# Embedding lookup and pairwise interaction: halves of 128 samples, wider lookups of nine tables, gram in two column tiles

## The reference, cut to what matters

```python
e = jnp.stack([tbl_0[ids[:, 0]], ..., tbl_26[ids[:, 26]]], axis=1)      # 2048 x 27 x 128
interactions = jnp.einsum('bfd,bgd->bfg', e, e)
x = interactions.reshape(B, F * F)[:, TRIL_IDX]                        # 351 pairs, i > j
h = jnp.concatenate([r_bottom_mlp_out, x, r_bottom_mlp_out], axis=1)     # 607 columns
h = jnp.maximum(h @ W_top1 + b_top1, 0.0)                              # 607 x 512
h = jnp.maximum(h @ W_top2 + b_top2, 0.0)                              # 512 x 256
y = h @ W_top3                                                         # 256 x 1
```

## Time and profile before

| | us |
|---|---|
| median of 3 runs | 481.43 (474.8 to 484.29) |
| the profiled execution | 476.27 |
| its span, first to last instruction | 474.5 |
| TensorE busy | 377.0 |
| GpSimd busy | 311.6 |
| VectorE busy | 255.4 |
| ScalarE busy | 155.2 |
| mean granted clock of TensorE | 0.939 of full |

### The profile page before, as it was taken

One profiled execution on the slowest core, in us unless ns is written; L12 is line 12 of the kernel. 1 busy time (PEld: TensorE's weight loads), 2 busy tenths in 40 slices (PEclk: granted clock), 3 DMA queues, 4 the chain that ended last, 5 costly groups with the idle time before them and its releaser, 6 DMA issues.

```text
span 474.5 us, 9001 instructions
## 1 busy us (share of the span) xinstructions
PE 377.0 (79%) x3732; PEld 343.9 (72%) x3732; DVE 255.4 (54%) x577; ACT 155.2 (33%) x199; POOL 311.6 (66%) x324
## 2 busy tenths in 40 slices
PE   0360686899898989898889889988989898976717
PEld 0360676888797879887788788878978797856616
DVE  0672863974498348835593549542974488310310
ACT  1312044224431453044404432333324531331411
POOL 5777557877777777777777777777777777720000
PEclk9965797999999999999999999998999999997967
DMA  6457512132224222422242222322242222210000
GB/s 157 152 178 205 162 32 71 42 133 68 67 67 137 67 66 64 141 68 62 63 143 59 66 69 74 128 65 71 65 136 66 67 67 59 67 37 4 1 16 0
DMA packets 24817, 38.69 MB, mean 82 GB/s; under 512 B 9436, under 2 KB 17125, under 8 KB 24776
## 3 DMA queue, kind: packets, MB, share of 16 engines
q0 software_dynamic: 10240, 20.99, 15.6%
q1 hardware_dynamic: 14536, 17.12, 12.1%
HBM read 35.00 MB, written 0.01 MB: 74 GB/s over the span
## 4 chain that ended last, share of the span: by engine, by line
PE 36%; DVE 24%; DMA 12%; issue 11%; POOL 10%; ACT 4%; SPq 3%; DVEq 0%
DVE mask L422 19%; PE gram_bank L531 11%; POOL rows L203 10%; PE mlp_bank L545 7%; PE col_bank L492 6%; DMA pairs<-in_tbl 6%; PE col_bank L506 6%; PE mlp_bank L556 5%; DVE pairs L455 3%; DMA rows<-in_tbl,idx 3%; SPq L229 3%; DMA rowid<-in_row_of_chunk 2%; ACT eT L322 2%; ACT pairs L334 1%; DVE eT L446 1%
## 5 line engine op out<-in xcount | busy, mean ns | idle before, releaser
L203 POOL DMA_INDIRECT rows<-in_tbl,idx x320 | 311.4, 973 | 107.1 <-issue 104.2
L492 PE MATMUL col_bank<-mask,parts 125*128 125x256 f32 x896 | 120.9, 294 | 49.8 <-DVE mask L422 48.4
L492 PEld LDWEIGHTS col_bank<-mask,parts 125*128 125x128 f32 x896 | 114.7, 200 | 57.0 <-issue 53.7
L422 DVE TENSOR_SCALAR mask<-hot_f,rowid 125x256 fp32r<-125x256 f16 x448 | 136.5, 374 | 0.1
L531 PE MATMUL gram_bank<-eT 128*58 128x52 f32 x2048 | 117.9, 218 | 13.5 <-issue 9.3
L531 PEld LDWEIGHTS gram_bank<-eT 128*58 128x58 f32 x2048 | 114.0, 135 | 19.9 <-issue 14.8
L446 DVE COPY eT<-col_bank 128x512 f32<-128x512 f32 x56 | 59.1, 1055 | 84.1 <-PE col_bank L506 81.3
L322 ACT ACTIVATE eT<-col_bank 128x512 f32<-128x512 f32 (+1 forms) x56 | 55.2, 986 | 148.1 <-PE col_bank L492 106.3
L455 DVE COPY pairs<-gram_bank 26x416 f32<-26x416 f32 x64 | 55.4, 865 | 84.6 <-PE gram_bank L531 84.1
L334 ACT ACTIVATE pairs<-gram_bank 26x416 f32<-26x416 f32 x64 | 56.8, 887 | 83.2 <-PE gram_bank L531 82.8
L545 PE MATMUL mlp_bank<-x,w 126*128 126x256 f32 (+5 forms) x288 | 64.0, 378 | 15.3 <-DMA x<-pairs 15.3
(11 more groups left out here) (10 smaller groups left out, 10.6 us busy)
## 6 DMA issues: line engine op xcount, KB each, us to landing
hot_i<-in_hot_ids SPq DMA_DIRECT2D x8, 896.0 KB
rows<-in_tbl,idx POOLq DMA_INDIRECT x320
pairs<-in_tbl SPq DMA_DIRECT2D x7, 500.0 KB
x<-in_bottom SPq DMA_DIRECT2D x8, 128.0 KB
x<-pairs SPq DMA_DIRECT2D x16, 39.0 KB
x<-pairs SPq DMA_DIRECT2D x16, 34.5 KB
w<-in_w SPq DMA_DIRECT2D x1, 512.0 KB
w<-in_w_pairs SPq DMA_DIRECT2D x2, 252.0 KB
```

The lines of the kernel that those rows point to most:

```text
L203: pool.indirect_dma_start(out=rows[:, h, n * D:(n + 1) * D], out_offset=None, in_=tables[f], in_offset=bass.IndirectOffsetOnAxis(ap=idx[:, ...
L422: last = nc.vector.tensor_scalar(mask[0:ROWS, k % MASKS, c, :], hot_f[0:ROWS, k, :], rowid[0:ROWS, c:c + 1], None, ALU.is_equal)
L492: last = nc.tensor.matmul(col_bank[b][:, i * TILE:(i + 1) * TILE], parts[0:ROWS, k, part, c * D:(c + 1) * D], mask[0:ROWS, k % MASKS, c, : ...
```

## The change

The unit of work becomes the half of 128 samples. Nine tables are looked up by TensorE (eight of 1000 rows and one of 1250, ten chunks), 18 are gathered. A lookup covers up to 512 samples, so each table is looked up once in four halves; its result goes to `eH`, and ScalarE places each half's columns from there into `eT`, which now holds one half. Two or three tables are looked up per half, in turn. In the front the lookups are 128 to 512 samples wide.

The ring of gathered rows is released group by group. All ids of the gathers come in one load, those of the lookups one table at a time. There are three column banks and three gram banks. The first half's transposes stand between the last five front lookups. A gram set is two strips of 16 samples, alternately at output partitions 0 and 64; VectorE copies strip 0, ScalarE strip 1, with the inner loop along samples, and the transposed groups are copied with the inner loop along tables. `pairs` and `x` are laid out by halves, so a transfer to x has runs of 1536 bytes. A table is loaded as 112 and 13 rows. At the end the last two halves' layers are interleaved, and half of the last transfers to x are issued from ScalarE. Layers 1 and 2 otherwise stay in tiles of 256.

The diff, cut to its core:

```diff
-ONE_HOT = 7
...
+ROWS = 125
+SMALLEST = [f for f in range(F) if VOCAB[f] == 8 * ROWS]
+NEXT = [f for f in range(F) if VOCAB[f] == 10 * ROWS]
+HOT_TABLES = SMALLEST[:2] + NEXT[:1] + SMALLEST[2:]
+HOT = len(HOT_TABLES)
+GATHERED_TABLES = [f for f in range(F) if f not in HOT_TABLES]
 GATHERED = len(GATHERED_TABLES)
-ORDER = GATHERED_TABLES + ONE_HOT_TABLES
-TILE = 256
-TILES = B // TILE
+ORDER = HOT_TABLES + GATHERED_TABLES
+CHUNKS = [VOCAB[f] // ROWS for f in HOT_TABLES]
 HALF = 128
-CHUNKS = 8
...
+HALVES = B // HALF
+TILE = 2 * HALF
+WINDOW = 4
+WIDE = WINDOW * HALF
+OWN = [[0, 1, 2], [3, 4], [5, 6], [7, 8]]
 PARTS = 2
-MASKS = 4
+PIECE = 2
+PIECES = [n // PIECE for n in CHUNKS]
+MASKS = 8
+SLOTS = 3
 STAGES = 3
 PAD = 32
...
 PACK = 2
-SET = 32
+GRAM_ROWS = (PACK - 1) * PAD + F - 1
+COLUMNS = 64
+STRIPS = 128 // COLUMNS
+STRIP = 16
+SET = STRIPS * STRIP
 SETS = HALF // SET
-GROUP = 4
 X_CHUNKS = 3
...
+SPLIT = 112
...
+GROUPS = spread(GATHERED, 4)
+NG = len(GROUPS)
+RING = 2 * NG
...
+LAST = HALVES - 1
...
+BANKS = 3
...
+LOOKUPS = [(k, 0, m + 1) for m in range(WINDOW) for k in OWN[m]]
+FRONT = len(LOOKUPS)
+AFTER = []
+for h in range(LAST):
+    AFTER.append([len(LOOKUPS) + i for i in range(len(OWN[h % WINDOW]))])
+    LOOKUPS += [(k, h + 1, min(WINDOW, LAST - h)) for k in OWN[h % WINDOW]]
...
+EARLY = FRONT - NG
...
+FRONT_ORDER = [("lookup", n) for n in range(EARLY)]
+for g in range(NG):
+    FRONT_ORDER += [("transpose", 0, g), ("lookup", EARLY + g)]
...
+def on_scalar(fill):
+    return fill < len(FRONT_ORDER) or fill % 2 == 1
...
+        def transposed(h, g):
+            n = transpose_fill(h, g)
+            return eT[:, :, HOT + GROUPS[g][0]:HOT + GROUPS[g][0] + GROUPS[g][1]], \
+                col_bank[n % BANKS][:, 0:GROUPS[g][1] * HALF].rearrange("p (f s) -> p s f", s=HALF)
...
+        def pairs_of(s, t, j):
+            a = s * SET + t * STRIP
+            return pairs[0:F - 1, :].rearrange("p (g s) -> p g s", s=HALF)[:, :, a + j:a + STRIP:PACK]
+        def gram_of(b, t, j):
+            row = COLUMNS * t + PAD * j
+            return gram_bank[b][row:row + F - 1, :, j * (F - 1):(j + 1) * (F - 1)].rearrange("p q g -> p g q")
...
+            pool.wait_ge(idx_loaded, 16)
+            for h in range(HALVES):
+                for g, (first, size) in enumerate(GROUPS):
+                    before = h * NG + g - RING
+                    if before >= 0:
+                        n = transpose_fill(before // NG, before % NG)
+                        pool.wait_ge(col_full[n % BANKS], n // BANKS + 1)
+                    for i in range(size):
+                        f = first + i
+                        pool.indirect_dma_start(
+                            out=rows_of(h, g)[:, i * D:(i + 1) * D], out_offset=None, in_=tables[GATHERED_TABLES[f]],
+                            in_offset=bass.IndirectOffsetOnAxis(ap=idx[:, h, f:f + 1], axis=0),
+                        ).then_inc(gathered[(h * NG + g) % RING], 16)
...
+            def load_table(k):
+                src = tables[HOT_TABLES[k]].rearrange("(p c) d -> p (c d)", c=CHUNKS[k])
+                for a, b in ((0, SPLIT), (SPLIT, ROWS)):
+                    sp.dma_start(stage_of(k)[a:b, :], src[a:b, :]).then_inc(table_loaded[k % STAGES], 16)
...
+            def load_x(h, blocks):
+                for b in range(BANKS):
+                    sp.wait_ge(gram_copied[b], STRIPS * used((h + 1) * SETS, b))
+                for r in blocks:
+                    out, src = x_block(h, r)
+                    sp.dma_start(out, src).then_inc(x_loaded[h % 2], 16)
...
+            for h in range(HALVES):
+                for n in CASTS[h] if h < LAST else ():
+                    if n + 2 < len(LOOKUPS):
+                        load_hot_ids(n + 2)
+                if h % 2 == 0:
+                    load_bottom(h // 2)
+                    if h >= 4:
+                        store_y(h // 2 - 2)
...
+                load_x(h, range(0, len(BLOCKS), 2) if h == LAST else range(len(BLOCKS)))
+            store_y(TILES - 1)
...
+            def place_hot(h, m):
+                at, first, last = (h - m - 1) % WINDOW * HALF, OWN[m][0], OWN[m][-1] + 1
+                return nc.scalar.activation(eT[:, :, first:last].rearrange("p s f -> p f s"),
+                                            eH[:, first:last, at:at + HALF], ACT.Copy)
+            def place_early(h):
+                for b in range(BANKS):
+                    act.wait_ge(gram_full[b], used(h * SETS, b))
+                for m in range(WINDOW):
+                    if m != (h - 1) % WINDOW:
+                        place_hot(h, m)
...
+                if h < LAST:
+                    copy_lookup(AFTER[h][0])
+                copy_pairs(h)
+                if h < LAST:
+                    place_early(h + 1)
+                    for n in AFTER[h][1:]:
+                        copy_lookup(n)
+                    place_late(h + 1)
...
+            for b in range(BANKS):
+                act.wait_ge(gram_copied[b], STRIPS * used(HALVES * SETS, b))
+            for r in range(1, len(BLOCKS), 2):
+                out, src = x_block(LAST, r)
+                nc.scalar.dma_start(out, src).then_inc(x_loaded[LAST % 2], 16)
...
+            a, b, c = AFTER[0]
+            make_masks(a)
+            copy_pairs(0)
+            make_masks(b)
+            copy_lookup(a)
+            make_masks(c)
+            copy_lookup(b)
             dve.wait_ge(weights_loaded, 16 * WEIGHT_LOADS)
...
+            nc.vector.tensor_tensor(w1[:, X_CHUNKS, :], w1[:, X_CHUNKS, :], wb, ALU.add).then_inc(w1_summed, 1)
+            make_masks(AFTER[1][0])
+            copy_lookup(c)
+            make_masks(AFTER[1][1])
+            for h in range(1, HALVES):
+                for g in range(NG):
+                    copy_transposed(h, g)
+                if h == LAST:
+                    copy_pairs(h)
...
+                else:
+                    a, b = AFTER[h]
+                    if h + 1 < LAST:
+                        make_masks(AFTER[h + 1][0])
+                    copy_lookup(a)
+                    copy_pairs(h)
+                    if h + 1 < LAST:
+                        make_masks(AFTER[h + 1][1])
+                    copy_lookup(b)
...
+            def look_up(n):
+                k, _, wide = LOOKUPS[n]
+                fill = lookup_fill(n)
+                fill_free(fill)
...
+                for c in range(CHUNKS[k]):
+                    piece = pieces_to(n) + c // PIECE
+                    if c % PIECE == 0:
+                        pe.wait_ge(masks_made, piece + 1)
+                    for part in range(PARTS):
+                        last = nc.tensor.matmul(
+                            col_bank[fill % BANKS][:, 0:wide * HALF], parts[k][0:ROWS, part, c * D:(c + 1) * D],
+                            mask[0:ROWS, piece % MASKS, c % PIECE, 0:wide * HALF], start=(c == 0 and part == 0),
+                            stop=(c == CHUNKS[k] - 1 and part == PARTS - 1))
+                    if c == CHUNKS[k] - 1:
+                        last.then_inc(col_full[fill % BANKS], 1)
+                    elif c % PIECE == PIECE - 1:
+                        last.then_inc(masks_used, 1)
...
+                    for q in range(STRIP // PACK):
+                        for t in range(STRIPS):
+                            a = s * SET + t * STRIP + q * PACK
+                            last = nc.tensor.matmul(
+                                gram_bank[n % BANKS][COLUMNS * t:COLUMNS * t + GRAM_ROWS, q, 0:PACK * (F - 1)],
+                                eT[:, a:a + PACK, :].rearrange("p s f -> p (s f)")[:, 0:GRAM_ROWS],
+                                eT[:, a:a + PACK, 1:F], start=True, stop=True)
+                    last.then_inc(gram_full[n % BANKS], 1)
...
+            for what, *which in FRONT_ORDER:
+                if what == "lookup":
+                    look_up(*which)
+                else:
+                    if which[1] == 0:
+                        pe.wait_ge(ident_loaded, 16)
+                    transpose(*which)
             pe.wait_ge(pads_cleared, 1)
...
+            multiply_pairs(0)
+            for n in AFTER[0]:
+                look_up(n)
+            for h in range(1, LAST):
+                transpose(h, 0)
+                transpose(h, 1)
+                if h % 2 == 0 and h >= 4:
+                    layer3(h // 2 - 2)
+                if h % 2 == 1 and h >= 3:
+                    layer1(h // 2 - 1, [3])
+                for g in range(2, NG):
+                    transpose(h, g)
+                look_up(AFTER[h][0])
+                multiply_pairs(h)
+                for n in AFTER[h][1:]:
+                    look_up(n)
+                if h == 1:
+                    pe.wait_ge(weights_loaded, 16 * WEIGHT_LOADS)
+                    pe.wait_ge(w1_summed, 1)
+                if h % 2 == 0 and h >= 2:
+                    layer1(h // 2 - 1, range(3))
+                if h % 2 == 1 and h >= 3:
```

(32 more changed lines are left out.)

694 lines of the change are left out of this document (329 added, 365 removed).

## The result

The changed kernel takes 427.88 us (median of 4 runs, 425.64 to 435.16), the kernel before 478.88 beside it: ratio 0.895 [0.8853, 0.9047]. The profiled execution took 426.37 us, its span is 424.6. Forecast were 400 (388 to 440) and a span of 392. So it became faster by 10.5%, inside the range, but 28 us above the number and outside the 388 to 412 us that the first case alone had been given.

A forecast was written before the change was run, and what follows sets the result against it. GpSimd's issue of gathers was taken to bound: last gather at 368 us, rows landed at 369, tail 23.3, span 392, 394 as its own time; plus 4 for the median and 2 for ring stalls, 400 us (388 to 440).

The forecast's parts named there:

- the first case: The main forecast for the whole kernel, with every term as taken: 400 us, own range 388 to 412, chance 49%.
- What bounds: Steady part: GpSimd's issue of gathers still bounds, 22.5 us per half against 21.1 for TensorE.
- Gram gains nothing: Rival, 28%: gram in two column tiles gets no faster, TensorE takes 23.6 us per half, 434 us in all.
- The price of a gather: GpSimd's stream: 1.25 us per gather, 288 instead of 320 gathers, so 40.0 us less.
- the stream's end: Last gather on GpSimd: 366.5 us, or 371.8 with the unexplained 5.3 us; 368 was taken.
- Gram: TensorE per half: 128 gram instructions at 32 instead of 56 ns, 4.1 us instead of 7.2.
- Lookups: TensorE per half: 37 products of 512 columns at 225 ns, 8.3 us against 6.9 before.
- VectorE: VectorE per half: masks 11.3, fills 3.8 and pairs 3.6 us, together 18.7, under the gathers' 22.5.
- the rival in which it bounds: Rival, 7%: slow tables or VectorE's masks and strided copies set start and middle, 415 to 450 us, 425 taken.
- Front: Start of the kernel: tables faster than one per 4.2 us, last mask about 45 us, gram 0 near 49, against 63.6.
- Tail: From the last rows' landing at 369 us to the end: 23.3 us, against 55.5 for the last two halves before.

## Why the prediction was right, and where it was off

*What bounds.* Right: GpSimd's gathers bound after as before; 288 of them, no hole, idle 0.30 us before each. "Gram gains nothing" would have put holes at group starts and TensorE without waits. Neither is there, though its 434 us was nearer to the measured 427.9 than my 400.

*The price of a gather.* This is the step that failed. I took 1.25 us as a constant and called the gather of 6.28 us one "that no view explains", one single 5.3 us. VectorE's timeline beside it would have shown 5.9 us of work without a break, though with 67 gathers untouched in such rows that trace gave no rate for it. I predicted masks twice as wide and front masks in longer rows, and priced what VectorE itself needs for them, not what they do to GpSimd. The term was 366.5 to 371.8 us for the stream's end; the last gather starts at 395.5. With narrow masks behind the front it starts at 367.77, so the masks' columns there are shown to cost 27.7 us, 25.7 on one chip. The Trainium skill has a mechanism, in SBUF — State Buffer, Who interferes with whom: VectorE's second port pair is GpSimd's only one, a tensor_scalar in a two-port mode takes it for the whole instruction, and GpSimd can't write a gather's descriptors meanwhile. The traces agree with the direction. They differ on the duration: where gathers were long, they were held over 8 to 20 instructions, not one, and in other such rows they were not held at all. What decides that stays open. For a tensor_tensor the page has GpSimd's reads in the way and infers that the writing of descriptors is not; here a gather, whose ids are read from SBUF, lasted 20.26 us under compares and splits of two tensors, and no run separates the two.

*The range.* That 427.9 lies in it is in part luck. The first case's own range ended at 412; the part up to 440 was there for other cases, above all for a gram that gains nothing, and none of them happened.

*Gram.* Right: 32 ns taken, 27 measured, 3.4 us per half between first and last start. The rule that I weighed against it (the Trainium skill, TensorE: Matmul & The Clock Gate, Part 3, The mechanism: weight loads overlap only where the row group differs) would have kept 7.2 us; with two column tiles in one row group the pace halved, in both kernels, and within a strip it went back when the alternation went.

*Lookups.* 225 ns taken, 227 measured.

*VectorE.* Too dear: a 512-column mask 0.61 us taken, 0.40 measured; an emptied bank 1.05 taken, 0.71 measured; pairs 0.45 taken, 0.38 measured. I had doubled the 305 ns of 256 columns without a fixed part, though no two widths stood in the trace; and those 305 were a mean of 262 ns and a longer step, some 466 ns, at every fourth mask. It left VectorE at 54%, and the rival in which it bounds off the table.

*Front.* Tables 3.3 us apart where I needed under 4.2; last mask at 43.4 (45 forecast), gram 0 at 49.97 (49), transpose (1,4) at 72.5 (79). A wait that I hadn't seen: ScalarE's cast waits 7.2 us for ids that SP had queued behind the weights. It costs nothing here, since gathers run on.

*Tail.* 29.1 us from the last start, 25 forecast. The last group's rows are there at about 398.0 (2.5 us after issue), but TensorE is in layers 2 and 3 of tile 6 and comes at 400.74: 2.7 us. The transfers to x take 6.0 us (406.42 to 412.37), 4.6 forecast: two queues halved the issue (3.76 us instead of 7.28), and the way behind it took 2.2 us instead of 1.1.

The sum: 28.5 us of gathers and 4.1 of tail make 32.6, the difference between the spans of 424.6 and 392.

## What to carry to other kernels

Where GpSimd issues the gathers that bound, VectorE's work in SBUF is a cost of GpSimd: look at each long gather and at what VectorE does above it, and price a change in VectorE's rows of work by what it adds to gathers. A speedup of an engine that isn't the bound was worth nothing here (the gram's 53 us of TensorE), and in the kernel before it came with 13.7 us of later gathers. And a single outlier that no view of its own engine explains is worth one more view, that of its neighbour.

## What the runs showed of the hardware

- A gather took 20.26 us, 15.76 to 36.02 us, while VectorE's instructions followed each other without a break from 14.56 to 35.2 us. Such rows don't always hold a gather: in the kernel before 67 gathers lie wholly in rows of over 5 us of masks of 256 columns, none longer than 1.05 us.
- Under masks of 512 columns a gather that is not long takes some 0.13 us more than its 944 ns, under masks of 256 in the kernel before 2 ns.
- Two f32 products in column tiles 0 and 64 of one row group follow each other by 27 ns each, 53 ns in one tile.
- On two other chips a gram of 128 short instructions took 18 to 23 us instead of 3.6, issued 0.7 or 1.4 us apart while gathers ran, and both kernels were slower there. The granted clock is not where it starts: from 303 to 306 us, with holes already and TensorE busy 0.87 of 3 us, the clock is still 1.00 of full (2.4 GHz), and then it falls to 0.5 (1.2 GHz), where it is from 309 to 321 us. The cause is open; longer instructions before and behind it were not touched:

```profile
317.00:321.00 4.00, 2.25 (x41) 2.06 (x43) 1.53 (x5) 1.42 (x5) 0.00 (x0) 0.50 0.04 11
321.00:333.00 12.00, 12.00 (x80) 10.42 (x77) 5.38 (x13) 6.25 (x14) 0.32 (x1) 0.90 0.07 21
```
